# A four-layer decoder on one core: shared-key scores from stacked bfloat16 terms, and matrix-memory attention in one stage

## The reference

```python
# sublayer 5 (L1_ffn): 16 heads of 16 channels share one key and one value for each token
gating = softmax(x @ W_gate.T); idx = argmax(gating)
q, k, v = split(x @ W_qkv.T, 3)
k_shared = the head idx of k;  v_shared = the head idx of v, times max(gating)
att = einsum('bhqd,bkd->bhqk', q, k_shared) / sqrt(16)      # causal
y = softmax(att) @ v_shared

# sublayer 10 (L3_xattn): matrix memory, q = x, k = v = the context
ig = cat(q, k, v) @ Wi + bi;  fg = cat(q, k, v) @ Wf + bf    # 16 gates each
F = cumsum(log_sigmoid(fg));  log_D = F[s] - F[t] + ig[t]    # causal
C = (q @ k.T / sqrt(16)) * exp(log_D - max(log_D))
h = (C / max(|sum C|, exp(-max))) @ v
out = (h - mean) / sqrt(var + eps) * ln_scale                # over the 16 channels of a head
```

## Time and profile before

| what | value |
|---|---|
| median of 3 runs | 2043.39 us (2041.53 to 2047.3) |
| the profiled execution: its time | 2044.2 us |
| the profiled execution: its span in the trace | 2042.2 us, so 2.0 us lie around it |
| TensorE busy | 1663.7 us (81%) |
| VectorE busy | 1330.9 us (65%) |
| ScalarE busy | 1052.0 us (52%) |
| GpSimd busy | 605.5 us (30%) |
| mean granted TensorE clock | 0.869 of full speed |
| shared-key sublayer | 1160.5 to 1299.6 us of the span |
| matrix-memory sublayer with its layer norm | 1802.0 to 1977.2 us |

### The profile page before, as it was taken

The page is one execution under the profiler, slowest core; times in us unless marked ns, Lnnn a source line. Parts: engine busy times, 40 slices in busy tenths (PEclk is TensorE's granted clock), DMA queues, the critical chain, the costliest instruction groups (busy, mean ns, idle before and its releaser), DMA issues. The chain is left out here.

```text
span 2042.2 us, 28328 instructions
## 1 busy us (share of the span) xinstructions
PE 1663.7 (81%) x9541; PEld 1041.5 (51%) x9541; DVE 1330.9 (65%) x2650; ACT 1052.0 (52%) x2070; POOL 605.5 (30%) x499
## 2 busy tenths in 40 slices
PE   7967899999997897999559799864999777358924
PEld 3743466666776535666446567452222434217712
DVE  3766877676764347885477556348999657924467
ACT  2013556555643147985248467325998522415525
POOL 0405342232200008994041050004980000407610
PEclk9979999999999998999879799887555668688959
DMA  4000000000000101110000000007999600020000
GB/s 203 27 1 26 1 1 1 1 1 1 1 1 0 59 22 42 49 45 11 16 1 2 27 1 2 24 32 193 183 184 185 119 5 5 0 83 1 1 0 21
DMA packets 163006, 80.64 MB, mean 39 GB/s; under 512 B 155280, under 2 KB 156432, under 8 KB 161200
## 3 DMA queue, kind: packets, MB, share of 16 engines
q1 hardware_dynamic: 162720, 78.46, 15.9%
q10 hardware_dynamic: 144, 0.39, 0.0%
HBM read 39.44 MB, written 1.11 MB: 20 GB/s over the span
## 5 line engine op out<-in xcount | busy, mean ns | idle before, releaser
L1213 POOL TENSOR_TENSOR ss_u<-dx,b_rows 128x512 f32<-128x512 f32 x128 | 159.1, 1277 | 242.3 <-POOLq L181 226.3
L2094 ACT ACTIVATE qc_p<-qc_s,qc_bias,sq 128x1024 int16<-128x1024 f32 x128 | 154.0, 1203 | 16.9 <-DVE qc_bias L2060 6.6
L1295 DVE TENSOR_TENSOR_SCAN ss_h<-ss_decay,ss_u 128x512 f32<-128x512 f32 x128 | 146.5, 1203 | 24.4 <-PE ss_ht L1253 18.5
L932 ACT ACTIVATE gq_p<-gq_s,gq_bias,gq_rq 128x512 f32<-128x512 f32 x128 | 98.4, 773 | 119.0 <-DVE gq_bias L1002 118.9
L2058 DVE TENSOR_REDUCE qc_mx<-qc_s 128x1 f32<-128x1024 f32 x128 | 155.4, 1214 | 4.8 <-PE qc_s L1993 4.8
L865 POOL TENSOR_TENSOR gq_xw<-gq_x,weights 128x512 f32<-128x512 f32 x48 | 67.9, 1414 | 297.2 <-ACT gq_x L892 296.5
L1993 PE MATMUL qc_s<-kT,qT 64*128 64x512 bf16 x256 | 130.8, 618 | 14.4 <-ACT qc_p L2094 7.1
L1267 PE MATMUL ss_acc<-ss_hc,consts 128*128 128x512 f32 x256 | 131.0, 594 | 0.0
L800 PE MATMUL gq_s<-gq_KT,gq_QT 128*128 128x512 f32 x256 | 121.4, 597 | 3.6 <-ACT gq_p L932 3.6
L822 PE MATMUL gq_o<-gq_pT,gq_V 128*128 128x256 f32 x512 | 121.2, 379 | 1.4 <-DVE gq_pT L1036 1.4
L999 DVE TENSOR_REDUCE gq_mx<-gq_s 128x1 f32<-128x512 f32 x128 | 88.2, 691 | 43.6 <-PE gq_s L800 43.1
(11 more groups left out here) (579 smaller groups left out, 4078.5 us busy)
## 6 DMA issues: line engine op xcount, KB each, us to landing
b_rows<-b_rows SPq DMA_DIRECT2D x16, 512.0 KB, 3.6
weights<-in_weights SPq DMA_DIRECT2D x1, 6152.0 KB, 17.5
weights<-in_weights SPq DMA_DIRECT2D x1, 5248.0 KB, 16.7
weights<-in_weights SPq DMA_DIRECT2D x1, 3072.0 KB, 10.8
weights<-in_weights SPq DMA_DIRECT2D x1, 2156.0 KB, 7.5
qc_pT<-qc_p SPq DMA_TRANSPOSE x128, 3.3
weights<-in_weights SPq DMA_DIRECT2D x1, 1410.0 KB, 9.1
weights<-in_weights SPq DMA_DIRECT2D x1, 1282.0 KB, 5.5
```

The source lines that it names most:

```text
L932: nc.scalar.activation(pr[c % 2][:, t, :], sc[t][:, :], ACT.Exp, bias=bias[:, c, t:t + 1], scale=rq[b % 2][:, t, u:u + 1], accum_out=sm[:, ...
L1213: nc.gpsimd.tensor_tensor(u_in[i % 3][:, :], dx[:, m, hf * HT:hf * HT + HT], rows.rows[c % 2][:, n % rows.NEACH, :], ALU.mult).then_inc(in ...
L1295: nc.vector.tensor_tensor_scan(h[group % 2][:, m, :], decay[i % 2][:].rearrange("p b t -> p (b t)"), u_in[i % 3][:, :], 0.0, ALU.mult, ALU ...
L2094: nc.scalar.activation(pi[i % R][:, :], sc[i % 3][:, :], ACT.Exp, bias=bias[:, i:i + 1], scale=sq[:, t, h:h + 1], accum_out=sm[:, i:i + 1] ...
```

## The change

In the shared-key sublayer:

- The query product now gives tokens on the partitions, one tile at a time (256 columns). ScalarE stores it in float32 (`qf`), then writes its bfloat16 rounding three times (`first_term`); GpSimd subtracts (`rest_of`); ScalarE writes the rounded rest three times (`second_term`); GpSimd writes the third term twice (`third_term`). Eight parts of 16 channels stand for one head, 128 in all. SP turns each tile by two DMA transposes of 1024 columns into `qT`, in bfloat16.
- VectorE writes the key in the matching eight parts (`key_terms`), TensorE turns it in bfloat16, two tiles at a time, and ScalarE stores it. `km`, `repeat` and GpSimd's masks are gone.
- A head's scores are then two bfloat16 products over all 128 partitions.
- The copies to `prT` are shared: even heads by ScalarE, odd heads by VectorE (`store_turned`), with one semaphore each. `outputs`, `out_turns`, `store_out` and `finish` run one head later.

In the matrix-memory sublayer: both gates in one product of 48 columns; the seven stages become one; running sums in two halves of 512 tokens; ScalarE instead of VectorE copies the values; `memory_norm` is worked batch by batch, its first three batches' steps spread over the loop on VectorE (`memory_steps`, `variance_steps`), the rest behind it; the layer norm is that of Finish. The products, exponentials and weightings of the 64 heads are as before. GpSimd's comparisons are spread around the masks and the scaling by ln_scale (`weigh`).

The diff, cut to its core:

```diff
-        with stage(g, "sh_logits ... (25 names) " + Finish.NAMES)
+        with stage(g, "sh_logits ... (33 names) " + Finish.NAMES)
-            def query(j):
-                m, n = j // 2, j % 2
-                if j >= 2:
-                    nc.tensor.wait_ge(qstored, j - 1)
+            def query(t):
+                if t >= 2:
+                    nc.tensor.wait_ge(qstored, t - 1)
                 for k in range(2):
-                    last = nc.tensor.matmul(ptb[j % 2][:, :], wqkv[:, k, m * P:m * P + P], g.XT[:, k, n * 512:n * 512 + 512],
+                    last = nc.tensor.matmul(ptb[t % 2][:, 0:256], g.XT[:, k, t * P:t * P + P], wqkv[:, k, 0:256],
...
+                if h == 0:
+                    nc.tensor.wait_ge(kstored, b + 1)
                 for t in range(2):
+                    if h == 0:
+                        nc.tensor.wait_ge(qout[(2 * b + t) % 4], 32 * (b // 2 + 1))
-                    nc.tensor.matmul(s, qT[:, h // 8, b * S + t * P:b * S + t * P + P],
-                                     km[:, h % 8, b * S:b * S + P * (t + 1)], start=True, stop=False)
+                    nc.tensor.matmul(s, qT[:, 2 * b + t, h, :], kT[:, 2 * b:2 * b + t + 1, :], start=True, stop=False)
...
             def outputs(i):
-                nc.tensor.wait_ge(copied, 4 * i + 4)
+                for parity in copied:
+                    nc.tensor.wait_ge(parity, 2 * i + 2)
...
+                for t in range(NT):
+                    query(t)
+                    if t + 3 < NT:
+                        select(t + 3)
+                    if t % 2 == 1 and t >= 3:
+                        turn_keys(t // 2 - 1)
+                turn_keys(B - 1)
+                pe.wait_ge(qstored, NT)
...
+                def store_query(t):
+                    act.wait_ge(queries, t + 1)
+                    if t >= 2:
+                        act.wait_ge(qmade, t - 1)
+                    nc.scalar.activation(qf[t % 2][:]..., ptb[t % 2][:, 0:256], ACT.Copy, scale=0.25).then_inc(qstored, 1)
+                def first_term(t):
+                    act.wait_ge(qstored, t + 1)
+                    nc.scalar.copy(qs[t % 4][:, :, 0:3, :], qf[t % 2][:]...).then_inc(qfirst, 1)
+                def second_term(t):
+                    act.wait_ge(qrest, t + 1)
+                    nc.scalar.copy(qs[t % 4][:, :, 3:6, :], qf[t % 2][:]...).then_inc(qsecond, 1)
                 for t in range(NT + 1):
+                    if t < NT:
                         store_query(t)
+                        first_term(t)
                     if t >= 1:
+                        second_term(t - 1)
+                    if t % 2 == 0 and t >= 4:
+                        store_keys(t // 2 - 2)
+                store_keys(B - 1)
...
+                def rest_of(t):                                   # GpSimd
+                    pool.wait_ge(qfirst, t + 1)
+                    nc.gpsimd.tensor_tensor(qf[t % 2][:], qf[t % 2][:], qs[t % 4][:, :, 0, :], ALU.subtract).then_inc(qrest, 1)
+                def third_term(t):
+                    pool.wait_ge(qsecond, t + 1)
+                    nc.gpsimd.tensor_tensor(qs[t % 4][:, :, 6:8, :], ..., ALU.subtract).then_inc(qmade, 1)
...
+                for t in range(NT):                               # SP
+                    sp.wait_ge(qmade, t + 1)
+                    for c in range(2):
+                        sp.dma_start(qT[:, t, 8 * c:8 * c + 8, :], qs[t % 4][:, 8 * c:8 * c + 8]..., transpose=True).then_inc(qout[t % 4], 16)
...
-                dve.wait_ge(kstored, NT)
+                dve.wait_ge(kstored, B)
...
+                    if u >= 5 and u % 2 == 1 and u - 4 < U:
+                        store_turned(u - 4)
+                    if u >= 6 and (u - 6) % 4 == 3 and u - 6 < U:
+                        store_out((u - 6) // 4)
```

More of the change, by code:

```diff
@@ new lines, in _ @@
+            @block.tensor
+            def _(pe):
+                gate_products(0)
+                gate_products(1)
+                turn_gates(0)
+                pe.wait_ge(gstored, 2)
+                pe.wait_ge(parts_made, 1)
+                turn_gates(1)
+                pe.wait_ge(parts_made, 2)
+                pe.wait_ge(ahead_sum, ahead.count)
+                ahead.total(pot[:].rearrange("p t h d -> p (t h d)")[:, 0:ahead.ngroups], ahead_total)
+                for i in range(U + 6):
+                    if i < U:
+                        scores(i)
+                    if i >= 2 and (i - 2) % 4 == 3 and i - 2 < U:
+                        outputs((i - 2) // 4)
+                    if i >= 4 and (i - 4) % 4 == 3 and i - 4 < U:
+                        out_turns((i - 4) // 4)
+                fin.turn(0)
+                fin.turn(1)
@@ new lines, in sum_weights, with store_values @@
+                def sum_weights(first, last):
+                    for i in range(first, last):
+                        if i >= 1:
+                            act.wait_ge(ahead_sum, i)
+                        nc.scalar.activation(ahead.low[0][:], ahead.items[i][0], ACT.Abs,
+                                             accum_out=ahead.part[:, i:i + 1]).then_inc(ahead_sum, 1)
+                def store_values(t):
+                    nc.scalar.copy(v[:, t, :, 0:16], ctok[:, t, :].rearrange("p (h d) -> p h d", h=16)).then_inc(v_made, 1)
@@ new lines, in _ @@
+                store_values(0)
+                store_values(1)
+                for u in range(U + 3):
+                    if u < U:
+                        exponents(u)
+                    if u < 6:
+                        store_values(u + 2)
+                    if u >= 3 and (u - 3) % 4 == 3 and u - 3 < U:
+                        store_out((u - 3) // 4)
+                    if u in (33, 49, 65):
+                        square((u - 33) // 16)
+                root(0, slice(0, 3))
+                square(3)
@@ L2601, in _ @@
+                root(1, slice(3, 4))
+                fin.root(0)
+                fin.store(0)
+                fin.root(1)
+                fin.store(1)
             @block.vector
             def _(dve):
-                link = Count(dve, chain)
-                nc.vector.memset(v[:, :, :, 16:17], 1.0).then_inc(ones_made, 1)
-                dve.wait_ge(ctx_in, 16)
-                for t in range(NT):
-                    last = nc.vector.tensor_copy(v[:, t, :, 0:16], ctok[:, t, :].rearrange("p (h d) -> p h d", h=16))
@@ L2735, in gated_ahead @@
+                invert(0, slice(0, 3))
+                result(0)
+                for _ in memory_steps(3):
+                    pass
+                result(1)
+                variance_steps(3)
+                fin.variance(0)
+                result(2)
+                invert(1, slice(3, 4))
+                result(3)
+                fin.variance(1)
+                fin.normalise(0)
+                fin.normalise(1)
 def gated_ahead(g, W, ctx, arrived):
@@ L3689, in program @@
             arrived = 16 * got if i < last else None
+            free = spans[i][1], width - spans[i + 1][1] if i < last else width
+            g.gap = region[:, free[0]:free[1]] if i % 2 == 0 else None
             if i in FUSED:
```

517 lines of the change are left out of this document (332 added, 185 removed).

## The result

The changed kernel takes 2027.28 us (median of 4 runs, 2022.68 to 2027.97) against 2042.46 (2038.28 to 2047.3): ratio 0.9912, 95% interval 0.9897 to 0.9927 (the ratio on record; the plain quotient of the two medians is 0.9926). It is faster by some 0.8%, clear of the noise, and by less than half of what was forecast (2009, range 1998 to 2024). The profiled execution took 2027.44 us, its span is 2025.1; the span before was 2042.2, so 17.1 us less, where the working gave 35.3.

A forecast was written before the change was run, and what follows sets the result against it. The prediction took TensorE to bound both loops, with one engine at a time in the matrix memory's start and end. Shared-key -5.3 us and matrix memory -30 gave -35.3 us, so 2009 us, range 1998 to 2024.

The forecast's parts named there:

- What bounds the kernel before: TensorE sets the shared-key loop at 1.416 us a head; matrix-memory loop also TensorE's, its start and end 85.7 us.
- The shared-key loop, 1.15 us a head: Shared-key loop: 63 heads at 1.15 us, 72.5 us against 89.2, a gain of 16.7, bounds 1.07 and 1.30.
- 0.2 us late: Shared-key loop: scores after the wait for VectorE's copy and `store_out` arrive 0.2 us late; four heads take 4.5 us.
- Rival 1: Shared-key loop gives its gain back: 1.3 us a head and late start, +5 there, total 2019; chance 0.20.
- VectorE's floor of 1.08 us: Shared-key loop: VectorE, busiest once it makes half the copies, needs at least 1.08 us a head.
- rival 2: Shared-key loop runs at VectorE's floor and the start costs 8 us: total 2001; chance 0.10.
- The start: Shared-key start: one query tile every 3.4 us, first row maximum at 1202.2, 8.9 us later than before.
- the 2 us for it: Shared-key loop: 2 us added for the first heads, as TensorE's clock will be at the lower level.
- The matrix memory: Matrix-memory sublayer: first score 20.8 us earlier, loop 89.5 us plus 0.5, end 26; -30 us, between -25 and -33.
- The tail: End of the matrix-memory stage: 20 us of VectorE, 2.7 for turning and storing, 3.5 to clear semaphores, 26 in all.
- Rivals 3: Shared-key loop: clock stays at 1.2 GHz, about 1.7 us a head, total 2044, no change; chance 0.05.
- 4: Matrix-memory loop: clock stays low, about 2.3 us a head instead of 1.3, +64 us, total 2073; chance 0.03.

The follow-up runs named there:

- experiment 3: Changed kernel with all 64 copies of transposes on ScalarE again, none on VectorE: 2001.99 us, ratio 0.9802 to the kernel before.
- experiment 2: Changed kernel with VectorE's copy of an odd head's transposes ahead of the two maxima of its step: 2004.89 us, ratio 0.9807 to the kernel before.
- experiment 4: Changed kernel with TensorE's turns one head later, VectorE's copy still behind the maxima: 2019.65 us, ratio 0.9881 to the kernel before.
- experiment 6: Changed kernel with VectorE's copy ahead of the maxima, plus both layer-norm roots ahead of the first half's stores: 2001.25 us, ratio 0.9797 to the kernel before.
- experiment 8: Changed kernel with unread TensorE fillers in the matrix-memory tail: products 2021.23 us, float32 transposes 2020.75, products up to the last sublayer 2023.11.

## Why the prediction was wrong, and where it was right

**What bounds the kernel before: right.** TensorE set the shared-key loop: with its float32 scores gone and the copies where they were, the loop goes from 1.42 to 1.02 us a head (experiment 3).

**The shared-key loop, 1.15 us a head: wrong, and the step that cost most** (63 x 0.153 = 9.6 us of the 18 that are missing). The step that failed is the overlap: I took the wait for VectorE's copy as hidden, and made `outputs` the stall. I saw that each parity has one buffer and that the turns wait for VectorE's copy, but in the sum it stands once for four heads and as "0.2 us late". The runs showed a circle, which is run through for each odd head, twice in four. Read from the timeline, it takes 0.15 us from the copy's end to the turns, 0.25 from there to the next scores, 0.5 from the scores to the maxima, 0.5 for the maxima and 0.55 for the copy, so 1.95. Twice that, plus about 1.0 for outputs and 0.35 for `out_turns`, is 5.25 us, against 5.23 in the timeline (maxima at 1240.21 and 1245.44). The outputs matter only since they stand inside this circle. Experiments 2 and 4 open it at two different places, experiment 3 takes it away; in all three the loop falls, with the outputs where they were. Rival 1 had the size of the loop right (1.3 us a head) and named the waits of each parity on an engine of its own; what I put against it, "in the hand schedule the extra waits overlap", was what failed.

**The prices: right where rows gave them.** 0.55 us for VectorE's copy (0.548), 1.16 for GpSimd's third term (1.153), 0.84 for the three copies of a term (0.83). The DMA transposes were hidden, as forecast, as long as there are two query buffers. VectorE's floor of 1.08 us was 1.04 in experiment 2, so the loop of rival 2 was one change in the order of two instructions away.

**The start: right.** 8.1 us later, forecast 8.9. The low clock came, but the 2 us for it did not show: the granted clock was 0.50 to 0.54 until 1208, and the first heads were no slower than the rest (63 heads at 1.303 us on average, 5.23 / 4 = 1.31 in the timeline at full clock), since the loop waits for other things. From the last maximum to the next sublayer it took 1.2 us more, not 0.5. The sublayer comes to +2.0 against -5.3, so 7.3 us worse: 9.6 of the loop, less these 2 and the 0.8 of the start, and 0.7 more at the end, which adds up to 7.5.

**The matrix memory: right in kind, 4.6 us too good.** The first score was 0.9 us late: TensorE's turning of the second half's gates waits for ScalarE's first floor (8.51 us), which stands behind the sums of weights, and the product over the sums stands behind that turning. The loop was exact. The tail was 3.5 us longer than its 26: I did not read ScalarE's order, where the second root stands behind the first half's two stores (2.3 us, experiment 6), one addition took 1.68 us instead of 0.69 while GpSimd's comparisons ran beside it (1.0 us), and the end of the stage, from ScalarE's last copy on, took 4.0 us instead of 3.5. Luck helped in the start: VectorE's running sums only just hide behind the sums of weights, since its last term is written at 1829.6 and the product starts at 1830.2. The forecast had 1.3 us of room there and the sums ended by 1824.5. The Trainium skill, "GPSIMD Engine Reference", section 1, says that GpSimd's SBUF interfaces are shared with VectorE, with contention for instructions with two SBUF inputs; the row of 1.68 us is such an instruction and agrees (0.69 us for its like at 1937.76, with GpSimd idle). It began at 1927.57, beside a GpSimd instruction of two inputs (1927.54 to 1928.69). VectorE's product of two inputs at 1926.77 ran beside a GpSimd instruction of one input and took 0.69, so not every GpSimd instruction slows such a row.

**The rest of the span: not in the sum at all.** The forecast put no term for it, and gave no reason. The unchanged sublayers took 6.4 us more in this execution, 5.2 of them the last one. In the eleven other executions with the new memory stage the last sublayer took 66.0 to 68.5 us, against 65.0 and 65.1 in the two with the old one, so as an estimate some 2 us belong to the change and 3 to that execution. TensorE's clock came back 27 us into it, against about 12 before and about 16 with the old memory stage and new shared key (65.1 us). With fillers it came back about 4 us into it, and the sublayer still took 66.0. So the clock alone does not order them. What of the 2 us is the clock and what is not stays open.

**Rivals 3 and 4 did not come.** The granted clock is 1.00 in the shared-key loop beyond 1210, and 0.98 on average in the memory loop. The Trainium skill, "TensorE: Matmul & The Clock Gate", Part 4, says that a transpose does not count towards the clock as a product does; the durations it gives there are of bfloat16 ones. Here the granted clock rose from 0.50 to 1.00 under float32 transposes alone (experiment 8). For these transposes the measurement decides against the rule; bfloat16 ones were not tested alone.

## What to carry to other kernels

When a loop is shared between two engines, don't add up loads; write down each buffer's circle (who frees it, what stands behind the one that waits, what stands ahead of the one that frees it) and count how often it is run through. Try to put an operation that frees a buffer ahead of the other work of its step: here moving one copy past two maxima took 17.5 us off the sublayer, where the new scores without that move had gained nothing. Before work is moved from a busy engine, look whether it would still be the busiest after the other edits: here ScalarE had the room, and the sharing was not needed (1.024 us a head without it). And read the order of every engine in a tail, not only of the busiest one.

## What the runs showed of the hardware

- TensorE's clock comes back at a different time in executions of the same code: from 140 to 160 us of the span the granted clock was 0.76 in the changed kernel and 0.91 in experiment 3, and the sublayers ahead of the change end 5.8 us apart over all executions (1161.8 to 1167.6). How much of these 5.8 us is the clock was not worked out. The last sublayer takes 66.0 to 70.2 us behind the new stage. Stage by stage, differences of 2 to 3 us are not the edit's unless the edit's own rows show them.
- Float32 transposes of a constant tile, with nothing else on TensorE, brought the granted clock from 0.50 (1924 to 1925) to 1.00 (from 1926) and kept it there for the 12 us that they went on.
- ScalarE has two starts of exponentials and one of a 384-column copy in 0.975 us when it does not wait (copies start at 1224.52, 1225.49 and 1226.48 in experiment 3), while their durations are 0.47, 0.37 and 0.48 in the changed kernel, 1.32 in all: the records of neighbours overlap by a quarter. So the sum of the durations overstates what a full engine needs.
